# Token mixer: probabilities stay fp32 and move through half arrays, split q and k are stacked by way of DRAM

## What is computed

```python
x = ...                                       # (128, 96, 512) float32
ch = qkv.shape[1] // 3                        # 32
q, k, v = jnp.split(qkv, 3, axis=1)           # each (128, 32, 512)
scale = 1.0 / np.sqrt(np.sqrt(ch))
weight = jnp.einsum('bct,bcs->bts', q * scale, k * scale)
weight = jax.nn.softmax(weight, axis=-1)      # over the 512 keys
h = jnp.einsum('bts,bcs->bct', weight, v)     # (128, 32, 512)
```

## Time and profile before

| | |
|---|---|
| median of three runs | 2807.41 us |
| profiled execution | 2800.67 us |
| its span | 2798.9 us |
| mean granted TensorE clock | 0.921 |
| busy share of the span | TensorE 83%, VectorE 69%, ScalarE 56%, GpSimd 40% |
| transfer engines, share of 16 | 21.2% |
| first and last copy of a mixer tile | 83.2 and 781.0 us |

### The profile page before, as it was taken

How to read it: one execution, slowest core, us unless ns; L and a number is a source line. 1 busy time by engine, 2 the same in 40 slices (tenths; PEclk the granted TensorE clock), 3 DMA queues, 4 the chain that set the end, 5 groups by cost and what they waited for, 6 DMA issues and landing times. The chain is left out here.

```text
span 2798.9 us, 53432 instructions
## 1 busy us (share of the span) xinstructions
PE 2316.2 (83%) x18020; PEld 1371.8 (49%) x18020; DVE 1936.9 (69%) x3306; ACT 1567.7 (56%) x2502; POOL 1111.3 (40%) x1093
## 2 busy tenths in 40 slices
PE   5877777666849898954899999689998699999998
PEld 2655555555736565632444444256665244444443
DVE  5766666666759998966744457467776788878873
ACT  3666666666835555545732246255554566666663
POOL 2545555455634444411410015133332455555552
PEclk8878888788979999976999999899999899999999
DMA  3222222222225121101211113322221111111101
GB/s 89 77 71 79 77 78 79 76 79 78 57 88 174 60 64 60 57 31 48 81 59 65 49 59 98 99 65 79 77 76 56 43 36 46 43 38 45 42 31 46
DMA packets 122042, 185.80 MB, mean 66 GB/s; under 512 B 20645, under 2 KB 47877, under 8 KB 121914
## 3 DMA queue, kind: packets, MB, share of 16 engines
q1 hardware_dynamic: 121914, 184.21, 21.2%
HBM read 116.78 MB, written 41.94 MB: 57 GB/s over the span
## 5 line engine op out<-in xcount | busy, mean ns | idle before, releaser
L295 DVE TENSOR_REDUCE tm_negmax<-tm_s 128x1 f32<-128x512 f32 x512 | 343.5, 682 | 244.2 <-PE tm_s L379 239.6
L208 POOL TENSOR_TENSOR tm_plo<-tm_prob,tm_phi 128x512 f16<-128x512 f32 x256 | 323.6, 1268 | 360.9 <-ACT tm_phi L251 360.8
L244 ACT ACTIVATE tm_prob<-tm_s 128x1024 f32<-128x1024 f32 x256 | 266.0, 1039 | 253.9 <-PE tm_s L389 252.7
L379 PE MATMUL tm_s<-tm_qk 96*128 96x512 f16 x512 | 228.3, 447 | 207.4 <-DMA tm_qk<-tm_xs 190.6
L1994 PE MATMUL f_part<-f_xhi,gu 128*128 128x512 f16 x704 | 270.0, 384 | 14.5 <-ACT f_firstg L1815 4.3
L1994 PE MATMUL f_part<-f_xlo,gu 128*128 128x512 f16 x704 | 269.2, 382 | 0.0
L2016 PE MATMUL f_pz<-dn,f_ghi 128*128 128x512 f16 x704 | 216.8, 383 | 27.1 <-ACT f_zc L1847 27.1
L389 PE MATMUL tm_s<-tm_qk 98*128 98x512 f16 x512 | 224.9, 439 | 3.6 <-ACT tm_prob L244 2.5
L1784 POOL TENSOR_TENSOR f_firstg<-f_firstg,f_secondg 128x512 f32<-128x512 f32 x88 | 148.6, 1689 | 198.3 <-DVE f_secondg L1890 198.3
L251 ACT CAST tm_phi<-tm_prob 128x512 f16<-128x512 f32 (+1 forms) x256 | 215.2, 841 | 0.0
L606 POOL CAST a_v<-a_qkv 128x128 f16<-128x128 f32 x64 | 18.6, 291 | 380.3 <-PE a_bankO L985 372.0
(11 more groups left out here) (214 smaller groups left out, 7089.2 us busy)
## 6 DMA issues: line engine op xcount, KB each, us to landing
tm_qk<-tm_xs SPq DMA_DIRECT2D x384, 64.0 KB, 2.6
tm_xqk<-in_x SPq DMA_DIRECT2D x64, 256.0 KB
a_hin<-h SPq DMA_DIRECT2D x64, 256.0 KB, 2.6
a_hres<-h SPq DMA_DIRECT2D x64, 256.0 KB, 2.7
h<-a_hout SPq DMA_DIRECT2D x64, 256.0 KB, 2.1
f_hin<-h SPq DMA_DIRECT2D x64, 256.0 KB, 3.1
f_hres<-h SPq DMA_DIRECT2D x64, 256.0 KB, 2.8
tm_xv<-in_x SPq DMA_DIRECT2D x32, 256.0 KB
```

Source lines behind the costliest of these rows:

```text
L208: pool.tensor_tensor(plo[b][:, j, :], prob[b][:, j, :], phi[b][:, j, :], ALU.subtract).then_inc(plo_pool, 1)
L244: nc.scalar.activation(prob[b][:, 2 * h:2 * h + 2, :], s2[:, h, :, :], ACT.Exp, scale=SCALE).then_inc(exp_done, 1)
L295: nc.vector.tensor_reduce(negmax[u][:, m:m + 1], s1[:, m % 2, :], AX.X, ALU.max, negate=True).then_inc(max_done, 1)
L379: nc.tensor.matmul(s1[:, m % 2, :], qk[u][0:KS, 0, b, i * P:(i + 1) * P], qk[u][0:KS, 1, b, :], start=True, stop=True).then_inc(s1_ready, 1)
```

## The change

The host hands the input over in two arrays, q and k as 4096 rows of 1024 numbers, and the values with the tokens in rows. The probabilities stay fp32 and are the moving operand: for each key block a product of 512 columns, whose stationary operand is 64 columns (32 channels of values and 32 columns of ones); of two sequences one fills output partitions 0 to 63 and the other 64 to 127 (`sum_values`). A group of four such products stands after slots 3, 7, 11 and 15. The output is then in its final layout with its denominator beside it. It is copied (`sums_out`), the denominators go by a transfer to 128 partitions (`denominators`), are inverted, are written to DRAM (`inverses`), read back by a transfer that repeats each row on 64 partitions (`inverse_rows`), and GpSimd multiplies (`normalise`).

The split q and k are written to DRAM (`spill`, three transfers of 256 KB) and read back stacked (`stack`, two of 384 KB). Maxima are turned and sent for each pair of sequences. The first scores have three banks and a lead of 14 slots; the turned maxima use the same banks.

```diff
-    LEAD, LAG = 7, 12
+    HALF = SLOTS // 2
+    USES = SLOTS + 2
+    BANKS = 3
+    LEAD = 14
+    E = B * T // P
...
-        s1 = ctx.enter_context(nc.psum_tensor("tm_s1", [P, 2, T], F32))
+        s1 = ctx.enter_context(nc.psum_tensor("tm_s1", [P, BANKS, T], F32))
+        o = ctx.enter_context(nc.psum_tensor("tm_o", [P, T], F32))
...
-        VALUES_AT, TOKENS_AT, MAXIMA_AT = 6, 14, 10
+        MAXIMA_AT = {11: 0, 3: 1}
+        VALUES_AT = {7: 0, 11: 1, 15: 2, 3: 3}
...
+        def unit(i):
+            pair, half, q = i // 4, i % 4 // 2, i % 2
+            return 2 * pair + q, half
...
+        def place(m):
+            return 0 if m == 0 else m + 1 if m < 9 else m + 2
+        def turned(pair):
+            return 1 if pair else 10
...
                     wait_alone(sp, sp_passed, xlo_done, t - 1)
+                    sp.dma_start(xqk[u][:, :, :], qk_dram[bass.ds(t * P, P)]).then_inc(qk_in[u], 16)
+            def load_values(t, u):
+                if inside(t, TILES):
+                    wait_alone(sp, sp_passed, pv_done, 4 * (t - 1))
+                    sp.dma_start(vt[u][:, :, 0:C, :].rearrange("p j c b -> p j (c b)"),
+                                 vt_dram[bass.ds(t * T, T), :].rearrange("(j p) n -> p j n", p=P)).then_inc(v_in[u], 16)
+            def spill(t, u, half):
+                if inside(t, TILES):
+                    wait_alone(sp, sp_passed, xlo_done, t + 1)
+                    for pair in range(2):
+                        wait_alone(sp, sp_passed, stacked[u][pair], 16 * half)
+                    for g, (lo, hi) in enumerate(((0, 2), (0, 3), (1, 2))):
+                        sp.dma_start(split_dram[u][g * C:(g + 1) * C].rearrange("c p b t -> b c p t"),
+                                     xs[u][:, lo:hi + 1:hi - lo, :]).then_inc(spilled[u], 16)
+            def stack(t, u, half, pair):
+                if inside(t, TILES):
+                    wait_alone(sp, sp_passed, spilled[u], 48 * (half + 1))
+                    wait_alone(sp, sp_passed, s2_ready, 8 * (t - 2) + 4 * pair + 4)
+                    b = slice(2 * pair, 2 * pair + 2)
+                    sp.dma_start(qk[u][0:KS, :, b, :], split_dram[u][:, :, b, :]).then_inc(stacked[u][pair], 16)
+            def maxima(t, u, pair):
+                if inside(t, TILES):
+                    wait_alone(sp, sp_passed, s1_read, use(t + pair, turned(pair)) + 1)
                     for part in range(2):
+                        sp.dma_start(qk[u][KS + part:KS + part + 1, 0, 2 * pair:2 * pair + 2, :]
+                                     .rearrange("o b (i t) -> o (b i) t", i=NT),
+                                     mrow[pair][:, part, :]).then_inc(mrow_in[pair], 16)
+            def denominators(t, u):
+                if inside(t, TILES):
+                    wait_alone(sp, sp_passed, nd_done, 2 * t + 2)
+                    wait_alone(sp, sp_passed, rden_done, t - 1)
+                    sp.dma_start(dens[u][:, :], nd[u][C::2 * C, :, :].rearrange("q p (a e) -> q (p a) e", e=E))\
+                        .then_inc(dens_in[u], 16)
+            def inverses(t, u, half):
+                if inside(t, TILES):
+                    wait_alone(sp, sp_passed, rden_done, t + 1)
+                    wait_alone(sp, sp_passed, rows_in[u], 16 * half)
+                    sp.dma_start(rden_dram[u].rearrange("b (a e) -> (b a) e", e=E), rden[u][:, :])\
+                        .then_inc(rden_out[u], 16)
+            def inverse_rows(t, u, half):
+                if inside(t, TILES):
+                    wait_alone(sp, sp_passed, rden_out[u], 16 * (half + 1))
+                    wait_alone(sp, sp_passed, norm_done, t - 1)
+                    sp.dma_start(rows[u][:, :, :].rearrange("p b t -> p (b t)"),
+                                 rden_dram[u].unsqueeze(1).broadcast_to([2, 2 * C, 2 * T])).then_inc(rows_in[u], 16)
...
             def store(t, u):
                 if inside(t, TILES):
+                    wait_alone(sp, sp_passed, norm_done, t + 1)
+                    for q in range(2):
+                        sp.dma_start(h_dram[bass.ds(t * P, P), :].rearrange("(p q c) t -> q c p t", q=2, c=C)[q],
+                                     hn[u][2 * C * q:2 * C * q + C, :, :]).then_inc(stored[u], 16)
...
                 n = 2 * k + u
+                stack(n + 1, 1 - u, k + u, 1)
+                inverse_rows(n - 2, u, k - 1)
+                spill(n + 2, u, k + 1)
+                maxima(n, u, 1)
+                denominators(n - 1, 1 - u)
+                load_values(n + 1, 1 - u)
                 load(n + 4, u)
                 store(n - 2, u)
+                stack(n + 2, u, k + 1, 0)
+                maxima(n + 1, 1 - u, 0)
+                inverses(n - 1, 1 - u, k + u - 1)
...
+            def normalise(t, u, half):
+                if inside(t, TILES):
+                    wait(pool, rows_in[u], 16 * (half + 1))
+                    wait(pool, stored[u], 32 * half)
+                    pool.tensor_tensor(hn[u][:, :, :], nd[u][:, :, :], rows[u][:, :, :], ALU.mult)\
+                        .then_inc(norm_done, 1)
...
+            def sums_out(t, u, pair):
+                if inside(t, TILES):
+                    wait(act, pv_done, 4 * t + 2 * pair + 2)
+                    wait(act, norm_done, t - 1)
+                    nc.scalar.copy(nd[u][:, pair, :], o[:, :]).then_inc(nd_done, 1)
...
+            def maxima_parts(t, pair):
+                if inside(t, TILES):
+                    p = turned(pair)
+                    turn = s1[0:HALF, p % BANKS, 0:P]
+                    wait(dve, s1_ready, use(t + pair, p) + 1)
+                    wait(dve, mrow_in[pair], 32 * t)
+                    nc.vector.tensor_copy(mrow[pair][:, 0, :], turn).then_inc(mhi_done, 1)
+                    wait(dve, mhi_done, 2 * t + pair + 1)
+                    nc.vector.tensor_tensor(mrow[pair][:, 1, :], turn, mrow[pair][:, 0, :],
+                                            ALU.subtract).then_inc(s1_read, 1)
+            def inverse_sums(t, u, half):
+                if inside(t, TILES):
+                    wait(dve, dens_in[u], 16 * (half + 1))
+                    wait(dve, rden_out[u], 16 * half)
+                    nc.vector.reciprocal(rden[u][:, :], dens[u][:, :]).then_inc(rden_done, 1)
...
+            def maxima(t, u, pair):
+                if inside(t, TILES):
+                    p = turned(pair)
+                    wait(pe, s1_read, use(t, place(HALF * pair + HALF - 1)) + 1)
+                    nc.tensor.transpose(s1[0:HALF, p % BANKS, 0:P], negmax[u][:, HALF * pair:HALF * (pair + 1)],
+                                        ident[:, :]).then_inc(s1_ready, 1)
...
+            def sum_values(t, u, half, r):
+                if inside(t, TILES):
+                    pair, h = r // 2, r % 2
+                    if r == 0:
+                        wait(pe, v_in[u], 16 * (half + 1))
+                    if h == 0:
+                        wait(pe, nd_done, 2 * t + pair)
+                    wait(pe, exp_done, 8 * t + 2 * r + 2)
+                    for j in (2 * h, 2 * h + 1):
+                        for q in range(2):
+                            b = 2 * pair + q
+                            last = nc.tensor.matmul(o[2 * C * q:2 * C * (q + 1), :], vt[u][:, j, :, b],
+                                                    prob[b][:, j, :], start=j == 0, stop=j == NT - 1)
+                    last.then_inc(pv_done, 1)
...
                     ahead, m = divmod(g + LEAD, SLOTS)
+                    pair = MAXIMA_AT.get(g)
+                    if pair is not None:
+                        maxima(n + 1 - pair, (u + 1 - pair) % 2, pair)
+                    scores_for_max(n + ahead, (u + ahead) % 2, k + (u + ahead) // 2, m)
                     scores(n, u, g)
+                    r = VALUES_AT.get(g)
+                    if r == 3:
+                        sum_values(n - 1, 1 - u, k + u - 1, r)
+                    elif r is not None:
+                        sum_values(n, u, k, r)
...
+    rden = nc.dram_tensor("rden", (2, 2, 1024), F32, kind="Internal").ap()
+    split = nc.dram_tensor("split", (2, 96, 2, 4, 512), F16, kind="Internal").ap()
+    token_mixer(nc, x[0], x[1], const["ident"], split, rden, h[0])
```

More of the change, by code:

```diff
@@ L324, in normalise @@
[L324 to L332 removed]
+                    p = place(m)
@@ L362, in _ @@
             pe.wait_ge(ident_in, 16)
-            pe.wait_ge(ones_set, 6)
-            def values_transposed(t, u, half):
-                if inside(t, TILES):
-                    wait(pe, v_in[u], 16 * (half + 1))
-                    wait(pe, norm_done, 2 * t - 1)
-                    for j in range(NT):
-                        last = nc.tensor.transpose(vT[:, j, :], xv[u][:, j * P:(j + 1) * P], ident[:, :])
-                    last.then_inc(vt_ready, 1)
+            pe.wait_ge(ones_set, 4)
             def scores_for_max(t, u, half, m):
@@ L406, in sum_values @@
-                    out = sums[b // 2][:, b % 2, i, :]
```

(28 more changed lines are left out.)

279 lines of the change are left out of this document (74 added, 205 removed).

## The result

The changed kernel takes 3039.39 us (median of four runs, 3037.54 to 3041.76) against 2807.12 us: 8.3% slower, ratio 1.0826, 95% interval 1.0807 to 1.0845. The forecast was 3019 us. The profiled execution took 3037.54 us, its span is 3035.7.

The account below looks back on a forecast made before the run. Queue order and engines per transfer bound the mixer's tile. Terms 36 + 40 + 848 + 42 + 30 make 996 us against 785, 211 more: 3012 profiled, 3019 median; own range 2960 to 3160, stated range down to 2725.

Parts of the forecast that it names:

- Both transfers narrow: Mixer transfers: spills get 4 engines, 9.4 us a tile; the inverses' broadcast gets 2, 10.3 us.
- Landing 22.5 us into the step, 7.8 us behind it: SyncE's step: pair 1's maxima land at 22.5 us, 7.8 us follow to the next step; period 30.3 us.
- The hole: TensorE at slot 8, the second scores of pair 1, stands 12 us waiting for maxima.
- The sum: Whole mixer: 36 + 40 + 848 + 42 + 30 = 996 us against 785; profiled execution 3012 us.
- What the other engines do: Per tile: GpSimd 5.7 us, VectorE at most 14.3, ScalarE 10.6; all under 15 and hidden.
- The fp32 group, 2.15 us: TensorE's group of four fp32 products: 0.86 us each, half arrays overlapping, 2.15 us a group, 8.6 a tile.
- Only the broadcast wide: Rival, spills narrow: maxima at 13.5 us, 19.8 us a tile, 2712 us; chance 0.10 for one narrow, either way.
- only the spills wide: Rival, broadcast narrow: maxima at 15.6 us, 23.4 us a tile, 2824 us; chance 0.10 for one narrow, either way.
- all wide: Rival: all transfers on sixteen engines or wait hidden; TensorE bounds at 16.8 us a tile, 2617 us; chance 0.11.
- Spread over sixteen at 25: Wide transfers use sixteen engines at 25 GB/s each; the two 384 KB restacks take 1.0 us each.
- SyncE as a plain queue: SyncE's order: maxima stand behind 1.0 + 10.3 + 9.4 us of restack, broadcast and spills, then need 1.7 us.

Follow-up runs that it names:

- the other order: Kernel with direct stacks, wide broadcast and six stack transfers on ScalarE, its four products a group reordered to both key blocks of one sequence first: 2607.24 us, against 2607.72 without.
- the run with ScalarE as issuer: Changed kernel with ScalarE instead of SyncE issuing the maxima, after exponentials 1 and 5: 2920.76 us, ratio 1.037 to the kernel before.
- the step with the maxima first: Changed kernel with SyncE sending the maxima of pair 1 before the broadcast and spills, both still narrow: 3060.19 us, ratio 1.0867 to the kernel before.
- one part alone: Kernel before with only the host's layout for q, k and values, loads led by 128: 2595.37 us, ratio 0.9221.

## Why the prediction was right

*Both transfers narrow*: shown. Stretches at a share of 0.14 and 0.25 stand in the trace, and widening one or the other removes exactly one of them. Until then no row had shown a transfer on two. By the rule of the Trainium skill that the prediction gives (DMA: Bandwidth & Descriptors, section Why a DMA increments its semaphore by 16 and not by 1), the leading 2 had to give two engines; the trace agrees, with 0.14.

*Landing 22.5 us into the step, 7.8 us behind it*: measured 22.6 and 7.7 in the tile shown. Four tiles from 320.84 to 443.74 us take 30.7 each, against 30.3. The hole is 12.8 us against 12. Inside the landing the parts came otherwise: GpSimd used the broadcast 14.1 us into the step (513.10 to 527.19), where I had 12. From 518 to 520 us, while the broadcast moved, the share was 0.25, which I read as the first spill beside it. By my reading that moves time from one term to the other and leaves their sum as it was; no run separates the two.

*The sum*: the profiled execution is 25.5 us above the 3012 worked out. The second scores start 2.6 us later, their steps take 949.7 us instead of 930, and from the last of them (988.3) to the last store (issued at 1020.1, landing a median of 3.7 later) are 35.5 us instead of 30. That is 27.8; the unedited stages give back 2.

*What the other engines do*: as costed, no engine near full, and VectorE at 0.68 us a maximum as before.

*The fp32 group, 2.15 us*: near the measured 1.93 (512.46 to 514.39), and by luck if the halves do not overlap. I took 0.86 us a product and overlapping halves. A quarter of 1.93 is 0.48 us a product, and the same time in the other order speaks for one after the other, though it does not prove it. That is the 0.49 us which 512 fp32 columns took in the earlier trace rows, before I doubled it for two records; then two errors cancelled. The change of tiling mode twice a group, which the sum left out, has 0.2 us if an fp32 record moves at the pace of an fp16 one (eight of 0.215 are 1.72); no run prices it. In this kernel little hung on it, since only one group stands behind the landing.

*The rivals' prices* were too low. "Only the broadcast wide" was put at 2712 and is 2814, "only the spills wide" at 2824 and is 2872, "all wide" at 2617 and is 2707. Three terms were mis-sized or put at nothing. "Spread over sixteen at 25" was 17 GB/s an engine in the stretch with the broadcast. Every transfer split to be wide costs SyncE 0.6 us more for each piece, which the sum left out: with both wide, the maxima were issued only 10.4 us into the step. And with only the broadcast wide I let TensorE go on at full clock behind the landing, 6.3 us to the next step; after a hole of 5.7 us the granted clock was 0.50 from 434 to 440 us, and the rest of the step took 8.2. The maxima of that run were used at 15.4 us instead of 13.5.

*SyncE as a plain queue*: I let it issue without delay and everything wait at the transfer engines. In fact SyncE was itself held for 12.1 us by three spills and could issue the maxima only then. The landing came out right since it is the same wait; that the issuer's order decides shows only in the run with ScalarE as issuer.

What stays open: how much each new wait of the step with the maxima first is worth. They are named above, but no run separates the late multiply, the late denominators and the late restack.

## What to carry to other kernels

Read the share of the transfer engines in a stretch where one transfer is alone: 0.14 or 0.25 names a transfer whose leading size is 2 or 4, and the bytes behind it in the same queue pay. Mend it with another layout before splitting it into pieces, because each piece takes its issuer some 0.6 us, and twelve of them are a new hole. Measure each part of a change on its own: here one part alone gained 219 us, and the sum of all lost 232.

## What the runs showed of the hardware

- An issue can hold its engine. The changed kernel's spill issues (count, duration min, median, max in ns):

```profile
L193 SPq DMA_DIRECT2D split<-tm_xs x96: 534/3729/9390, 8.4 to 926.2; - x96
```

  A plain load of 512 KB took SyncE 0.35 us in the kernel before with the host's layout, a wide piece of 64 KB 0.64 (7.67 / 12).
- Transfers issued by ScalarE passed those queued by SyncE: 5.4 us from issue to use, in the middle of 11.7 us of spill issues and with the older broadcast still on its way.
- Transfer engines moved about 25 GB/s each with two at work on the broadcast, 20 to 22 with four on the spills, and 17 with fifteen on a mix of both. The number at work does not explain the 17: in the changed kernel, with loads and a restack under way, all sixteen moved 391 GB/s, 25 each:

```profile
536.50:537.50 1.00, 1.00 (x4) 0.31 (x3) 0.69 (x1) 0.24 (x1) 0.00 (x0) 0.50 0.99 391
```

  The kinds of transfer differ between these stretches; no run says which property of theirs counts.
- Four fp32 products of 512 columns with 64 stationary columns took 1.93 us at full clock, 0.48 each, in either order of the halves.
